# Where a low half stands in VectorE's order, and four smaller reorderings, in a kernel of graph layers

## The reference, cut to what matters

```python
h = jnp.maximum(_layernorm(x), 0.0)
for l in range(3):                      # _L0_gnn_ref, x = h at first
    si, sj = x @ attn_w[l, :d], x @ attn_w[l, d:]
    scores = si[:, :, None] + sj[:, None, :] + attn_b[l]
    scores = jnp.where(scores >= 0, scores, 0.2 * scores)
    attn = softmax(jnp.where(mask, scores, -jnp.inf))
    h = layernorm(x + attn @ x, g1[l], beta1[l])
    ff = gelu(h @ W1[l] + b1[l], approximate=False) @ W2[l] + b2[l]
    x = layernorm(h + ff, g2[l], beta2[l])
# then x = x_in + that; h = relu(layernorm(x)); Wh = h @ W (256 x 256)
# e = leaky_relu(e_i + e_j), masked by adj, softmax, elu(attention @ Wh), added to x
```

## Time and profile before

| | |
|---|---|
| three runs, us | 2486.96, 2490.18, 2493.39; median 2490.18 |
| the profiled execution's own time | 2492.89 us, span 2491.2 |
| granted clock of TensorE, mean | 0.982 |
| PE busy | 2262.1 us, 91% |
| DVE busy | 1902.4 us, 76% |
| ACT busy | 1576.9 us, 63% |
| POOL busy | 1089.6 us, 44% |
| DMA | 128.55 MB, mean 52 GB/s |

### The profile page before, as it was taken

How to read it: one execution, slowest core, us unless ns; L and a number is a source line. 1 busy time by engine, 2 the same in 40 slices (tenths; PEclk the granted TensorE clock), 3 DMA queues, 4 the chain that set the end, 5 groups by cost and what they waited for, 6 DMA issues and landing times.

```text
span 2491.2 us, 41367 instructions
## 1 busy us (share of the span) xinstructions
PE 2262.1 (91%) x14623; PEld 1715.4 (69%) x14623; DVE 1902.4 (76%) x5107; ACT 1576.9 (63%) x2426; POOL 1089.6 (44%) x2056
## 2 busy tenths in 40 slices
PE   5899999998899999999999989999988999999987
PEld 4566667666676767776776767667666677666776
DVE  7677779658787788778887788877877776776865
ACT  5467566746566666675767566756656666756654
POOL 4344345453164434553354442735443453435611
PEclk9999999999999999999999999999999999999988
DMA  6312012101130112110211111301131010100000
GB/s 220 110 43 89 5 61 76 45 16 49 55 101 5 39 51 94 60 41 4 93 56 56 43 39 56 110 2 43 45 100 60 5 39 10 39 8 23 25 20 26
DMA packets 66221, 128.55 MB, mean 52 GB/s; under 512 B 12985, under 2 KB 53213, under 8 KB 62942
## 3 DMA queue, kind: packets, MB, share of 16 engines
q1 hardware_dynamic: 66014, 125.90, 15.1%
HBM read 111.20 MB, written 14.68 MB: 51 GB/s over the span
## 4 chain that ended last, share of the span: by engine, by line
PE 55%; DVE 26%; ACT 7%; issue 6%; POOL 5%; DMA 1%; SPq 0%; DVEq 0%; POOLq 0%; ACTq 0%
PE OB L1621 35%; PE FBB L1621 12%; DVE pw L1245 5%; DVE mj L1221 4%; PE RB L1621 3%; DVE gT L1259 3%; ACT nms L893 3%; DVE st L1112 2%; PE TH L1621 2%; DVE junk L1163 2%; POOL rs L636 1%; DVE xc L1139 1%; DVE xc L1126 1%; ACT FBB L865 1%; ACT L865 1%
## 5 line engine op out<-in xcount | busy, mean ns | idle before, releaser
L1621 PE MATMUL OB<-xx,pw 128*128 128x257 f32 x4096 | 952.5, 388 | 29.5 <-DVE xc L1139 15.5
L1621 PEld LDWEIGHTS OB<-xx,pw 128*128 128x128 f32 x4096 | 774.0, 193 | 158.2 <-DVE xc L1139 21.4
L1621 PE MATMUL FBB<-hT,wb 128*128 128x512 f16 x2304 | 563.7, 383 | 86.0 <-DVE gT L1259 85.6
L1621 PE MATMUL OB<-wb,gT 128*128 128x256 f16 x4608 | 569.6, 274 | 7.5 <-DVE gT L1259 7.5
L1621 PEld LDWEIGHTS OB<-wb,gT 128*128 128x128 f16 x4608 | 452.4, 99 | 137.7 <-DVE gT L1259 10.1
L631 POOL TENSOR_SCALAR ve<-mv 128x2 f32<-128x2 f32 x256 | 59.7, 233 | 1051.1 <-DVE mv L1115 1042.6
L865 ACT ACTIVATE FBB<-FBB,wc 128x512 f32<-128x512 f32 x384 | 253.0, 659 | 284.0 <-PE FBB L1621 282.9
L1259 DVE TENSOR_TENSOR gT<-FBB,gT 128x512 f16<-128x512 f32 x384 | 262.6, 684 | 211.7 <-ACT gT L870 211.3
L1621 PEld LDWEIGHTS FBB<-hT,wb 128*128 128x128 f16 x2304 | 212.6, 98 | 301.7 <-DVE gT L1259 104.0
L876 ACT ACTIVATE pw<-pw,sj 128x512 f32<-128x512 f32 x512 | 336.7, 712 | 68.2 <-DVE pw L1245 67.3
L654 POOL TENSOR_TENSOR xc<-xc,gb 128x256 f32<-128x256 f32 x384 | 292.5, 762 | 33.4 <-ACT xc L840 33.3
(11 more groups left out here) (132 smaller groups left out, 2307.0 us busy)
## 6 DMA issues: line engine op xcount, KB each, us to landing
wb<-w_scratch SPq DMA_DIRECT2D x19, 2048.0 KB, 7.9
adjst<-in_adj SPq DMA_DIRECT2D x56, 512.0 KB, 4.2
xx<-in_x SPq DMA_DIRECT2D x16, 512.0 KB, 5.7
nm<-in_L_gnn_W SPq DMA_DIRECT2D x6, 1024.0 KB, 8.5
gb<-in_L_gnn_g SPq DMA_DIRECT2D x48, 128.0 KB, 2.7
adjst<-in_x SPq DMA_DIRECT2D x6, 1024.0 KB, 10.7
out_x<-adjst SPq DMA_DIRECT2D x48, 128.0 KB, 1.7
pw<-in_adj SPq DMA_DIRECT2D x4, 1024.0 KB, 9.9
```

The source lines that it names most:

```text
L1621: return pe.matmul(o, lhsT, rhs, start=first, stop=last)
```

## The change

It has six parts, named A to F here.

A. On VectorE `g_low(k, 1)` now stands before the blocks, and block n does `g_low(k, n + 1)` behind the unit scores and before everything else of the block. Early scores of the GAT two steps on (AHEAD) stand in blocks 4 to 7 instead of 1, 3, 5, 7.

B. ScalarE does a gelu on one column at t = 6 of each FFN step, behind the high half of ht. ScalarE holds one set of functions at a time; with it the table of gelu is loaded there.

C. SHIFT_FE and SHIFT_FC have one mask fewer at position 7; it and those behind it stand at later positions.

D. In step 5 the GAT products come at blocks 2, 3, 4, 6 and go into RB, the parts on ScalarE and VectorE follow, and columns, maxima and masks of the next step are one position later.

E. For steps 30 and 31 the maxima, masks and units have earlier positions, and units 12 to 15 of step 30 other banks.

F. `elu_b` is gone. GpSimd's `final` adds both parts, one after the other; the −1 is folded into beta2 of the third layer by a small GpSimd instruction at the start of its affine (8 in all).

```diff
-MAX_FG = {19: (0, 1), 20: (2, 3), 21: (4, 5), 22: (6, 7)}
+MAX_FG = {20: (0, 1), 21: (2, 3), 22: (4, 5), 23: (6, 7)}
-MAX_TB = {3: (0,), 4: (1, 2), 5: (3, 4), 6: (5, 6), 7: (7,)}
+MAX_TB = {3: (0, 1, 2, 3), 4: (4, 5), 5: (6, 7)}
-SHIFT_FE = {6: (0, 1), 7: (2, 3), 11: (4,), 12: (5,), 13: (6,), 14: (7,)}
+SHIFT_FE = {6: (0, 1), 7: (2,), 10: (3,), 11: (4,), 12: (5,), 13: (6,), 14: (7,)}
...
+    if k == 30:
+        return {1: (8, 9, 10, 11), 2: (12, 13, 14, 15)}
+    if k == 31:
+        return {0: (12, 13, 14, 15)}
...
             def final(g, t):
-                pool.wait_ge(elu_sum, 8 * g + t + 1)
+                n = 8 * g + t + 1
                 v = x1_of(g)[:, t, :]
+                pool.wait_ge(elu_exp, n)
+                pool.tensor_tensor(out=v, in0=v, in1=vn[:, t % 2, :], op=ALU.add).then_inc(elu_sum, 1)
+                pool.wait_ge(elu_max, n)
+                pool.wait_ge(elu_sum, n)
                 pool.tensor_tensor(out=v, in0=v, in1=va[:, t % 2, :], op=ALU.add).then_inc(o_ready, 1)
...
                     if t in (4, 6):
                         ht_high(k, t // 2 - 2)
+                    if t == 6:
+                        act.activation(warm1[:, :], zero1[:, :], ACT.Gelu)
...
-                        if n in (2, 3, 5, 6):
-                            gat_values(gat, (2, 3, 5, 6).index(n))
+                        if n in (3, 4, 5, 7):
+                            gat_values(gat, (3, 4, 5, 7).index(n))
...
-            def elu_b(k, t):
-                n = 8 * ORDER[k][0] + t + 1
-                dve.wait_ge(elu_exp, n)
-                dve.wait_ge(elu_max, n)
-                dve.scalar_tensor_tensor(out=va[:, t % 2, :], in0=vn[:, t % 2, :], scalar=-1.0,
-                                         in1=va[:, t % 2, :], op0=ALU.add, op1=ALU.add)\
-                   .then_inc(elu_sum, 1)
...
+                g_low(k, 1)
                 for n in range(NF):
-                    if n > 0:
-                        g_low(k, n)
...
                     unit_scores(k, 8 + n)
+                    if 1 <= n < NF - 1:
+                        g_low(k, n + 1)
                     prepare(k, 8 + n)
...
-                    if k + 2 in AHEAD and n in (1, 3, 5, 7):
-                        scores(k + 2, n // 2)
+                    if k + 2 in AHEAD and n in (4, 5, 6, 7):
+                        scores(k + 2, n - 4)
...
-                        if n in (1, 2, 4, 5):
-                            gat_product(gat, (1, 2, 4, 5).index(n))
+                        if n in (2, 3, 4, 6):
+                            gat_product(gat, (2, 3, 4, 6).index(n))
```

More of the change, by code:

```diff
@@ L166, in prep_tables @@
     if k in GAT_FFN_LATE:
-        return dict(col=15, ct=16, s1=17, sj=18, row=MAX_FG, units=UNITS_FG, shift=SHIFT_FG)
+        return dict(col=16, ct=17, s1=18, sj=19, row=MAX_FG, units=UNITS_FG, shift=SHIFT_FG)
     if not is_gat(k):
@@ L191, in score_bank @@
     if q in RB_CARRY:
+        if q == 30 and u > 11:
+            return ("TH", "R1", "R0", "TH")[u - 12]
         return ("TH", "TP")[u % 2] if u in (8, 9, 12, 13) else ("R0", "R1")[u % 2]
@@ L197, in score_bank, with same_bank @@
     return ("R0", "R1")[u % 2]
+def same_bank(q, u):
+    return max((v for v in range(u) if score_bank(q, v) == score_bank(q, u)), default=None)
 def build(nc, x, adj, attn_w, attn_b, W1, b1, W2, b2, g1, beta1, g2, beta2, gatW, gata, out):
@@ L316, in build, with product_bank @@
         TPb = TPf.bitcast(bf16)
+        def product_bank(g, j):
+            return RB[:, HALF * (j % 2):HALF * (j % 2 + 1)] if g == 0 else THf
         BANK = {"TH": THf, "TP": TPf, "R0": RB[:, 0:HALF], "R1": RB[:, HALF:N]}
@@ L649, in affine @@
                     pool.wait_ge(s, 32 * (fi(k) + 1))
+                    if kind == LN2 and layer(k) == LAYERS - 1:
+                        pool.tensor_scalar(gb[:, 1, :], gb[:, 1, :], 1.0, -1.0, op0=ALU.mult, op1=ALU.add)\
+                            .then_inc(less_one, 1)
+                        pool.wait_ge(less_one, ORDER[k][0] + 1)
                 if kind == LN1:
@@ L741, in ffn_step @@
                         affine(LN2, k, 1)
-                    if n == (9 if k in GAT_FFN_LATE else 5) and k in SUM_AT:
+                    if n == (9 if k in GAT_FFN_LATE else 7) and k in SUM_AT:
                         node_sum(SUM_AT[k])
@@ L989, in ffn_step @@
                         ht_high(k, 2)
-                        if k not in GAT_FFN_LATE:
-                            gelu(k, 2)
+                        if k in GAT_FFN_LATE:
+                            gat_pair(gat, 0)
+                        gelu(k, 2)
                         normalise_pair(LN1, k, 3)
                     if k in GAT_FFN_LATE:
-                        if n in (1, 2, 3, 5):
+                        if n in (2, 3, 5):
                             gat_pair(gat, (1, 2, 3, 5).index(n))
@@ L1738, in spread_sj @@
                 if q in FREE_FB:
[L1739 to L1741 removed]
+                    pe.wait_ge(cT_done, q + 1)
+                    if q > 0:
                         pe.wait_ge(max_done, 8 * q)
@@ L1789, in gat_product @@
                 pe.wait_ge(ptl_done, 4 * g + j + 1)
-                pe.wait_ge(*th_after[-1])
+                if g > 0:
+                    pe.wait_ge(*th_after[-1])
+                elif j < 2:
+                    pe.wait_ge(x_done, 16 * GAT_STEP[0])
+                else:
+                    pe.wait_ge(wv_done, j - 1)
                 for i in range(2):
-                    o = THf[:, i * D:(i + 1) * D]
+                    o = product_bank(g, j)[:, i * D:(i + 1) * D]
                     rows = slice(i * P, (i + 1) * P)
@@ L1877, in gat_step @@
                     aggregate(k, t)
-                    prepare(k, t)
+                    if k != 30 or t != 2:
+                        prepare(k, t)
                     for u in carried(k).get(t, ()):
                         unit(k, u)
+                    if k == 30 and t == 2:
+                        prepare(k, t)
                     if gat is not None:
```

39 lines of the change are left out of this document (17 added, 22 removed).

## The result

The changed kernel takes **2524.42 us** (median of 4 runs, 2518.01 to 2527.02) against 2491.78 for the kernel before on the same chip (4 runs, 2486.96 to 2494.11): ratio **1.0133**, 95% interval 1.0117 to 1.0148, 32.6 us slower. I had forecast slower, 2500.5, with a range up to 2519: the sign holds, the size doesn't.

What follows compares the result with a forecast made beforehand. The kernel was taken as bound by TensorE, busy 2262.1 of 2491.2 us. Terms summed to +10 on the profiled 2492.9: 2503, or 2500.5 in the median's terms; own range 2491 to 2512, outer range 2458 to 2519.

Steps and rivals of the forecast that it cites:

- the mechanism of part A: Earlier low halves cut FBB's wait for gT (85.6 us), but overtaken VectorE work then waits behind them for gelu.
- Rival 1: The halves' gain isn't given back: faster, 2418 us in full, 2459 with half given back; chance 0.30.
- rival 2: Gains and losses cancel: gat_low costs once a step, not three times, so 28 becomes 14; 2486 us, chance 0.20.
- rival 4: The warm-up fails: another exp before gelu(0) makes the table load twice, +31 us on ScalarE; 2515 us, chance 0.03.
- The six steps, +28: FFN steps beside a graph attention (8, 12, 16, 20, 24, 28): 4.7 us longer each, +28 in all.
- step 12 stands for them: Step 12's working, 0.5 + 0.9 + 1.2 + 1.2 + 0.9 = 4.7 us, was applied to all six attention-side steps.
- rival 3: New waits in block 4 and before next aggregations slow the clock: 3.4 us more in six steps, 2521 us; chance 0.12.
- Steps 0, 4, 7, 23, −7: In these four steps front waits go and nothing binding is overtaken: −2, −1.9, −2, −1.3, together −7 us.
- The late steps, 0: Steps 1, 2, 3, 25, 26, 27: the wait before hidden(3) goes, but later row maxima and scores give it back; 0.
- Steps 9 to 22, +3.4: Steps 9, 13, 17, 21 lose +5 us through later residuals and clock; steps 10, 14, 18, 22 gain 1.6 from part F.
- in the sums above: Parts B and C got no term of their own; their gain was counted within the step sums through earlier low halves.
- Part D, +6: Step 5: front waits save about 5 us, but a later score chain and slower clock cost more; +6 net.

Runs made afterwards that it cites:

- e8: The changed kernel with the attention's low half (gat_low) ahead of the FFN's in blocks 5, 7, 9, 11 of the six steps: 2499.61 us.
- e1: The changed kernel with low halves back at the head of their blocks, all other parts and the early scores kept: 2447.78 us.
- e3: The kernel before with part A alone, and GpSimd's node sum in block 7: 2570.4 us.
- e12: The changed kernel with gat_low and gat_edges ahead of low halves in the six steps, low halves 13 to 15 back in all steps: 2458.7 us.
- e10: The changed kernel with low halves back at the head of their blocks, except low half 1, alone ahead of block 0: 2438.95 us.
- e6: The kernel before with part D alone (order of step 5): 2487.60 us.

## Why the prediction was right in kind and wrong in size

*What bounds the kernel; the mechanism of part A.* Right. FBB's wait fell below 30, and the time came back where I had placed it: 3.48, 1.26 three times, 4.33. e8 took 24.8 us away where my working had 0.9 + 1.2 + 1.2 in six steps, 20. Rival 1 (nothing given back) is refuted by e1 and e3, rival 2 by e8, and rival 4 by the count of loads, 24 for gelu as before.

*The six steps, +28; it was +40.6.* This is the first mis-sized term. In step 12 itself the working held: counted from the step's start, hidden 6 stood 0.6 us later than before (I had said 0.5), the three transposes 1.4, 2.9 and 4.4 (1.4, 2.6, 3.8) and the end 5.4 (4.7). What failed is "step 12 stands for them", for two reasons. The first is the clock, which I kept out of the likeliest case, calling it rival 3. Step 8 has the same 3.48 us wait for scores. Around it, and behind that of step 12, the granted clock (the first number behind the brackets) and the hidden product behind the wait are:

```profile
781.00:787.00 6.00, 5.05 (x20) 2.82 (x21) 4.18 (x10) 3.14 (x5) 1.27 (x4) 0.50 0.00 1
...
782.35 2.77 PE L1638 MATMUL FBB<-hT,wb 128*128 128x512 f16 x6
```

```profile
1082.00:1090.00 8.00, 6.06 (x46) 4.26 (x47) 5.33 (x11) 5.46 (x9) 1.27 (x4) 1.00 0.01 2
...
1082.91 1.46 PE L1638 MATMUL FBB<-hT,wb 128*128 128x512 f16 x6
```

Six matmuls take 2.77 us at 0.50 and 1.46 at 1.00. Over the whole steps 8, 12 and 28:

```profile
730.30:827.60 97.30, 87.95 (x578) 65.91 (x578) 67.99 (x184) 59.46 (x95) 44.12 (x88) 0.96 0.11 36
1031.00:1126.80 95.80, 85.22 (x577) 64.71 (x577) 67.93 (x184) 59.44 (x95) 44.09 (x88) 1.00 0.11 37
2289.70:2393.30 103.60, 88.57 (x578) 66.13 (x578) 74.59 (x196) 64.75 (x103) 49.20 (x96) 0.95 0.09 24
```

Steps 8, 16 and 20 lost 1.3 to 1.5 us more than step 12, 4.3 together, all three with a granted clock below 1.00 where step 12 has 1.00. So rival 3 came true in three steps of six, for less than half its price of 3.4 each; that the measured 2524 lies next to its 2521 is luck.

The second reason is step 28. Up to hidden 15 it is 4.4 us late, like step 12; behind that it loses another 6.2, where step 12 loses 1.0. TensorE waits there for scores, where it didn't wait before, and ahead of the scores VectorE makes gat_edges for the last graph. VectorE, GpSimd and TensorE in the changed kernel, then the same edges in the kernel before:

```profile
2381.13 5.05 DVE L1318 SCALAR_TENSOR_TENSOR nm<-ident,dgm,nm 128x128 bf16<-128x128 f32 x8
2381.14 0.73 POOL L677 TENSOR_TENSOR xx<-xc,gb 128x256 f32<-128x256 f32 x1
...
2388.54 0.61 PE L1638 MATMUL RB<-identb,nms 128*128 128x128 bf16 x4 [5.74 <-DVE pw L1273]
```

```profile
2333.32 2.73 DVE L1290 SCALAR_TENSOR_TENSOR nm<-ident,dgm,nm 128x128 bf16<-128x128 f32 x8
```

The eight instructions take 5.05 us, where they took 2.73 before and the earlier trace rows has eight in 2.19; GpSimd runs its adds beside them. With part A alone (e3) it is 5.03, without early halves (e1) 3.07. So the early halves moved the edges beside GpSimd's adds. How the 5.74 us divide between that, low halves 14 and 15 and the clock, 0.95 over this step, no run separates: with the two back in place (e12) the edges took 5.55 and the wait was still 4.07.

*Steps 0, 4, 7, 23, −7; it was +3.5.* The step that failed was "the front waits go and nothing binding is overtaken". TensorE in step 23 of the changed kernel:

```profile
1901.99 0.32 PE L1737 MATMUL TP<-identb,c 128*64 128x128 bf16 x1 [4.08 <-DVE c L1219]
...
1928.24 1.03 PE L1638 MATMUL RB<-identb,nms 128*128 128x128 bf16 x8 [3.02 <-DVE M L1249]
```

These are a wait of 4.08 us for the columns c and one of 3.02 for a row maximum M; step 0 has the same pair, 3.56 and 3.02. The columns were not late: they came 1.0 us sooner in step 23 than before (51.9 us from its start for 52.9). TensorE came sooner still, and several short waits for halves (2.21 and less) with one of 1.06 for the columns became a single one. I had the gain of the front and not what it runs into. The row maxima did end 3.2 us later in the step, with low halves ahead of them. And the granted clock of step 23 was 1.00 before and 0.94 now.

*The late steps, 0; it was +2.8.* The mechanism held: the 2.81 us wait is gone, and step 25 waits 2.10 us for a row maximum instead. e10 shows what I had netted away: the wait of the earlier trace rows was nearly all to be had (2.5 us of step 25), by low half 1 alone.

*Steps 9 to 22, +3.4; it was 0.0.* The front gained 2.5 us (I had said 2.9), and the row maxima at the end cost 2.1 (2.5). What was wrong is the 1.7 for the clock behind the 4.33 wait. The clock did fall, the granted clock of steps 10, 14, 18 and 22 was 0.95 in three and 0.96 in one; but these steps are only 0.2 to 0.4 us longer than before, and as much longer in e1, where the wait is 1.90. The kernel before has waits of 0.43 and 0.61 us among the next tiles of step 10; in the changed kernel 80 matmuls run there without one. The step had room for slow matmuls.

*Parts B and C.* I let their gain be "in the sums above". It was 27.2 us by itself, and so hid as much of the price of A. My terms for the steps that both touch (+28, +5, 0, −7) make +26; with 27 taken out of them they come to an estimated 53 for A alone, where 76.6 was measured. A net term per step can't show that one of its parts is good and the other bad. Steps 8, 9, 12, 13, 16, 17, 20 and 21 gained 1.5 to 1.8 us each from the load (1283 ns) and the mask (1.1 us) that no longer stand before gelu(0). A drain of another 1.38 us for each switch, as the Trainium skill has it (ScalarE: Activation LUTs, "What ACT_TABLE_LOAD costs"), would have left the load no room at t = 6: in step 9 only 0.66 us of idle time are left behind it. No sign of it is seen; the one-column gelu starts 0.01 us after the load ends.

*Part D, +6; it was +2.7, and −2.1 in its step alone (e6).* I had said that the wait before the units would become the longer one. It did:

```profile
587.62 1.03 PE L1638 MATMUL RB<-identb,nms 128*128 128x128 bf16 x8 [10.97 <-DVE M L1249]
```

But it belongs to part A: with low halves 13 to 15 back in place (e12) it is 5.30 us and the step 4.1 us shorter, without early halves (e1) 4.76. *Part E, −16:* −16.5 in its steps, of which 13.4 are E's alone. *Part F, −4 and +0.3:* −2.0 in all (interval up to nothing), with −3.9 in steps 6 and 29.

The two terms that failed were short by 12.6 and 10.5 us, 23 of the 24.0 between my sum, 9.7, and +33.7; the rest (2.2 before step 0, 2.8 in the late steps, 2.3 in steps 6 and 29, 1.1 in 11, 15, 19; against them 3.4 in the pairs, 3.3 in step 5, 0.5 in 30 and 31 and the 0.3) nearly cancels.

## What to carry to other kernels

In an in-order queue an instruction that has to wait should stand no earlier than it can run: moved ahead, it turns its own wait into one for all it overtook. Before moving, list for each overtaken instruction who waits for it and how long it had to spare; here one low half of fifteen had nothing tight behind it, and moving only that gave 8.8 us where moving all cost 77. A wait taken away at the front of a step is won only if the next thing that TensorE needs is ready sooner too; in step 23 several short waits became one long one. And price the parts of a bundle apart, by pairs like e1 (all but the part) and e3 (the part alone): this one held 42 us of gain under a loss of 77.

## What was new of the hardware

In these traces a small VectorE instruction takes up to ten times its length while GpSimd is in a long one. Before step 0 of the changed kernel, with VectorE and GpSimd side by side:

```profile
29.87 1.80 POOL L825 TENSOR_TENSOR xc<-xc 128x768 f32<-128x768 f32 x1 [6.96 <-DMA hT<-in_L_gnn_W]
29.97 1.73 DVE L1259 TENSOR_TENSOR um<-s,M 128x4 f32<-128x4 f32 x1
...
31.73 0.54 DVE L1261 SCALAR_TENSOR_TENSOR um<-um 128x4 f32<-128x4 f32 x1
```

The 128x4 subtraction, 0.16 us otherwise, took 1.73, and ended with GpSimd's add of 1.80. In the kernel before, the same three stood a moment before GpSimd's and took 0.16 each. The edges' 5.05 us, beside GpSimd adds of 0.72 us one after the other, are the same thing; both kinds have two operands in SBUF. Over the whole trace of the changed kernel, the second of the three took 0.16 us in all 29 cases without a GpSimd instruction beside it, and 0.58 in the median of the 34 beside one of GpSimd's TENSOR_TENSOR. A low half, which has one operand in PSUM, took 0.69 in the median of both kinds. The Trainium skill says of this (GPSIMD Engine Reference, "Specifications") that the two share their SBUF interfaces, with contention where a VectorE instruction has two SBUF inputs, and these rows agree. I had named it for part F and let it move no term. It is one reason why an order that runs well in one step can cost more in another, as in step 28. The 2.2 us before step 0 go with it, since the third of the three ends 2.2 us later than before; they came and went among kernels that do the same there.
